# Loads from two queues, ternary weights ahead of the last head folds, and a fifth lane in the second layer of a post-norm decoder

## The reference

```python
x = _layernorm(x + _L0_attn_ref(x, weight, bias, decay_value))   # x @ (Wr + Wc) + bias; Wr, Wc upper triangular, made from powers of the decay
x = _layernorm(x + _L0_xattn_ref(x, ctx_512, Wq, Wkv_expand, Wout))  # 16 heads of 16 over 64 context rows, softmax
x = _layernorm(x + _L0_ffn_ref(x, router_w, gate_w, up_w, down_w, shared...))  # top 1 of 8 experts, and a shared expert
x = _layernorm(x + _L1_attn_ref(x, W_q, W_kv, W_o))     # FFT per head, L2 norm, cumulative sum over tokens, product, inverse FFT
x = _layernorm(x + _L1_xattn_ref(x, ctx_512, Wq, w_kc_q, w_kc_kv, W_qr, W_kr, Wo))  # 16 heads with rotary keys, softmax
x = _layernorm(x + _L1_ffn_ref(x, w_gate_up, w_proj))   # ternary weights, silu(gate) * up, rms norm
```

## Time and profile before

| | us |
|---|---|
| median of 3 runs (671.78 to 671.95) | 671.81 |
| the profiled execution, whole | 670.62 |
| its span, first to last instruction | 669.3 |
| PE busy, share of the span | 563.9, 84% |
| DVE busy | 477.3, 71% |
| ACT busy | 386.3, 58% |
| POOL busy | 378.5, 57% |

### The profile page before, as it was taken

One profiled execution on the slowest core, in us unless ns is written; L12 is line 12 of the kernel. 1 busy time (PEld: TensorE's weight loads), 2 busy tenths in 40 slices (PEclk: granted clock), 3 DMA queues, 4 the chain that ended last, 5 costly groups with the idle time before them and its releaser, 6 DMA issues. The chain is left out here.

```text
span 669.3 us, 14453 instructions
## 1 busy us (share of the span) xinstructions
PE 563.9 (84%) x5305; PEld 443.6 (66%) x5305; DVE 477.3 (71%) x1297; ACT 386.3 (58%) x826; POOL 378.5 (57%) x469
## 2 busy tenths in 40 slices
PE   3789998888798998906577999998999989999993
PEld 3566777777575655603345779786788777889982
DVE  3774757686578669549879665788688888777562
ACT  1767776766674554425544555682746747566552
POOL 3435374737751034259999896373654824444874
PEclk9999999999798999966769899999999999999997
DMA  7663222102553433261001010101000010000001
GB/s 231 191 213 88 76 71 74 49 2 84 164 168 116 137 103 116 72 181 40 28 26 35 1 32 3 32 1 33 1 7 27 2 32 1 1 1 3 1 17 47
DMA packets 50417, 41.96 MB, mean 63 GB/s; under 512 B 15514, under 2 KB 48796, under 8 KB 50332
## 3 DMA queue, kind: packets, MB, share of 16 engines
q1 hardware_dynamic: 48812, 36.85, 18.3%
q0 software_dynamic: 1536, 4.20, 1.9%
HBM read 31.72 MB, written 10.35 MB: 63 GB/s over the span
## 5 line engine op out<-in xcount | busy, mean ns | idle before, releaser
L1763 DVE TENSOR_TENSOR first<-bank,first 128x512 f16<-128x512 f32 (+3 forms) x141 | 75.5, 557 | 21.6 <-ACT first L1656 5.2
L2232 POOL TENSOR_TENSOR first<-first 128x512 f16<-128x512 f32 x44 | 51.8, 1180 | 33.9 <-ACT first L1650 27.1
L1039 PE MATMUL bank<-c_identity,first 128*128 128x128 f32 (+2 forms) x353 | 58.6, 281 | 14.4 <-ACT first L1589 3.2
L1039 PE MATMUL bank<-c_identity,wide 128*128 128x128 f32 (+3 forms) x203 | 35.8, 301 | 41.4 <-ACT wide L1589 20.7
L1032 PE MATMUL bank<-wide,first 128*128 128x256 f16 (+3 forms) x199 | 54.9, 286 | 4.7 <-DVE first L1763 2.4
L1039 PEld LDWEIGHTS bank<-c_identity,wide 128*128 128x128 f32 (+3 forms) x203 | 25.1, 151 | 48.3 <-ACT wide L1589 21.7
L1039 PEld LDWEIGHTS bank<-c_identity,first 128*128 128x128 f32 (+2 forms) x353 | 39.6, 139 | 23.8 <-ACT first L1589 4.2
L1033 PE MATMUL bank<-wide,first 128*128 128x256 f16 (+3 forms) x199 | 54.8, 285 | 0.0
L1034 PE MATMUL bank<-wide,first 128*128 128x256 f16 (+3 forms) x199 | 54.7, 285 | 0.0
L2210 POOL TENSOR_TENSOR first<-first,minus_half 128x2 f32<-128x2 f32 x30 | 22.0, 734 | 35.7 <-DVE first L1873 35.7
L1763 DVE TENSOR_TENSOR wide<-bank,wide 128x512 f16<-128x512 f32 (+3 forms) x57 | 35.1, 636 | 7.0 <-ACT wide L1629 2.2
(11 more groups left out here) (470 smaller groups left out, 2091.5 us busy)
## 6 DMA issues: line engine op xcount, KB each, us to landing
first<-sent_rows SPq DMA_DIRECT2D x20, 128.0 KB, 2.1
made_rows<-first SPq DMA_DIRECT2D x20, 128.0 KB, 1.7
wide<-in_L_xattn_Wq SPq DMA_DIRECT2D x9, 256.0 KB, 2.9
wide<-in_L_ffn_gate_w SPq DMA_DIRECT2D x8, 256.0 KB
wide<-in_L_ffn_up_w SPq DMA_DIRECT2D x8, 256.0 KB
wide<-in_L_ffn_down_w SPq DMA_DIRECT2D x8, 256.0 KB
wide<-in_L_xattn_Wo SPq DMA_DIRECT2D x16, 128.0 KB
wide<-in_L_ffn_w_gate_up SPq DMA_DIRECT2D x8, 256.0 KB
```

The source lines that it names most:

```text
L1039: last = nc.tensor.transpose(view[0:m, c0:c0 + n], src, kc["identity" if dt == F32 else "identity_bf"][0:n, 0:n])
L1763: return V.tensor_tensor(lo, whole, hi, ALU.subtract)
L2232: G.tensor_tensor(B.pl[r], B.pf, B.ph[r], ALU.subtract).then_inc(says("ex_l"), 1)
```

## The change

- **Loads.** A new part `ld_dv` loads the decay value and the steps on their own semaphore, first on SP; `pm_dv` and `pm_pow` wait for these two alone, `pm_diag` and `pm_b` for the seven transfers left in `ld_mix`. The copy of ones leaves `pm_pow` for a part `pm_one`. `ld_cross` and, for units 0 to 4, `ld` and `ld_ctx` are issued on ACT's queue; SP's remaining early loads are chained in a fixed order (constants, shared, spectrum, experts). The decay mask is bf16.
- **Turns.** The ternary weights come before the head folds 6 and 7.
- **Lane.** `LANES` is 5; the fifth lane lies over the stage buffers and the area `fifth`. The first unit in it, 12, waits in `gt`, `ld` and `ld_ctx` for `tb_tok`, all `fw_c` and all `ho_lo` (`staged`). Units take lane (u - 8) % 5.
- **Ternary scale.** Two DVE steps of `f_sc` become one.
- **Plan.** Several lengths are changed, and 60 passes are tried, not 30.

```diff
-LANES = 4
+LANES = 5
+STAGED = 4
-    c["decay_mask"] = (j >= i).astype(np.float32)
+    c["decay_mask"] = bf(j >= i)
-EARLY_FOLDS = 4
+EARLY_FOLDS, MIDDLE_FOLDS = 4, 6
-         + [("h", n) for n in range(EARLY_FOLDS, NPREP)] + [("f", n) for n in TERNARY])
+         + [("h", n) for n in range(EARLY_FOLDS, MIDDLE_FOLDS)] + [("f", n) for n in TERNARY] + [("h", n) for n in range(MIDDLE_FOLDS, NPREP)])
+def staged(u):
+    return NB <= u < NB + LANES and u - NB >= STAGED
-    p.add("ld_mix", 0, 0, "SP", 450, (), -10)
+    p.add("ld_dv", 0, 0, "SP", 90, (), -11)
+    p.add("ld_mix", 0, 0, "SP", 320, [("ld_dv", 0, 0)], -10)
-    p.add("ld_cross", 0, 0, "SP", 140, (), -8)
+    p.add("ld_cross", 0, 0, "ACT", 140, (), -8)
-    p.add("ld_const", 0, 0, "SP", 600, (), -7)
+    p.add("ld_const", 0, 0, "SP", 600, [("ld_mix", 0, 0)], -7)
-    p.add("pm_diag", 0, 0, "DVE", 87, [("pm_pow", 0, 0)], -10)
+    p.add("pm_diag", 0, 0, "DVE", 102, [("pm_pow", 0, 0), ("in_mix", 0, 0)], -10)
-            p.add("ld_e", 0, i, "SP", 140, freed, rank)
+            p.add("ld_e", 0, i, "SP", 140 if i > 1 else 230, freed if i > 1 else [("ld_spec", 0, 0)], rank)
-            p.add("f_sc", 0, i, "DVE", 160, [("f_16", 0, i)], rank)
+            p.add("f_sc", 0, i, "DVE", 170, [("f_16", 0, i)], rank)
-        p.add("ld", u, 0, "SP", 45, [old("res", 2), old("rt_xs")], -9.5 + 0.01 * u if u < FIRST else k)
+        p.add("ld", u, 0, "ACT" if u < FIRST else "SP", 45, [old("res", 2), old("rt_xs")], -9.5 + 0.01 * u if u < FIRST else k)
+        if staged(u):
+            gate += [("tb_tok", 0, 0)] + [(name, 0, n) for name in ("fw_c", "ho_lo") for n in range(NPREP)]
-    p.settle(8, 30)
+    p.settle(8, 60)
-            pool_ = [couples[n - 2].back()]
+            pool_ = [couples[n - 2].back()]
+        else:
+            pool_ = [wide.back(STAGES), fifth.back()]
-        return k.B[u % FIRST if u < NB else FIRST + u % LANES]
+        return k.B[u % FIRST if u < NB else FIRST + (u - NB) % LANES]
+        if staged(u):
+            sp.wait_ge(*done("tb_tok", 0))
+            for i in range(NPREP):
+                sp.wait_ge(*done("fw_c", 0, i))
+                sp.wait_ge(*done("ho_lo", 0, i))
+    def load(out, in_, s):
+        nc.scalar.dma_start(out, in_).then_inc(s, 16)
-        dve.step(V.tensor_scalar(W.sc16, W.sc32, 1.0 / GRP, None, ALU.mult))
-        dve.step(V.tensor_scalar(W.sc16, W.sc16, 1e-8, None, ALU.max))
+        dve.step(V.tensor_scalar(W.sc16, W.sc32, 1.0 / GRP, 1e-8, ALU.mult, ALU.max))
+        pool.wait_ge(*done("tb_tok", 0))
+        if staged(u):
+            for n in range(NPREP):
+                pool.wait_ge(*done("fw_c", 0, n))
+                pool.wait_ge(*done("ho_lo", 0, n))
```

More of the change, by code:

```diff
@@ L847, in turns_of, with later_turns @@
     return len(range(n, NB, FIRST))
+def later_turns(n):
+    return sum((u - NB) % LANES == n for u in range(NB, 2 * NB))
 def sync_program(k, sp):
@@ L955, in ld @@
                 sp.wait_ge(*done("ln_x", u - LANES, 3))
-            load(B.y, unit_rows(k.x_mid, u - NB), dma["x"][u % LANES])
+            load(B.y, unit_rows(k.x_mid, u - NB), dma["x"][(u - NB) % LANES])
     def ld_ctx(u, g):
-        B, s = k.lane(u), dma["ctx"][u % FIRST if u < NB else u % LANES]
+        B, s = k.lane(u), dma["ctx"][u % FIRST if u < NB else (u - NB) % LANES]
         if u >= NB:
@@ L992, in st @@
         sp.wait_ge(*done("ln_x", u, 3))
[L993 to L995 removed]
+        load(unit_rows(k.out, u - NB), k.lane(u).x, dma["lane_out"][(u - NB) % LANES])
+    parts = {f.__name__: f for f in (ld_dv, ld_mix, ld_const, ld_shared, ld_spec, ld_zero, ld_tab, ld_e, ld_h, ld_f, ld, ld_ctx, st_mid, x_ld,
                                      x_st, st)}
@@ L1482, in summed, with ld_cross, ld, ld_ctx @@
         return summed_rows(k, u, n)
+    def load(out, in_, s):
+        nc.scalar.dma_start(out, in_).then_inc(s, 16)
+    def ld_cross(u, g):
+        for out, name in ((pre.raw_t[0], "L0_xattn_Wq"), (pre.raw_t[1], "L0_xattn_Wout"), (pre.raw_kv, "L0_xattn_Wkv_expand")):
+            load(out, k.A[name].rearrange("(c p) n -> p c n", p=P), dma["cross"])
+    def ld(u, g):
+        load(lane(u).x, k.A["x"][u:u + 1, :, :].rearrange("a (t p) n -> p (a t) n", p=P), dma["x"][u])
+    def ld_ctx(u, g):
+        for half in range(2):
+            load(lane(u).ctx[half * L:(half + 1) * L, :], k.A["ctx_512"][u, :, :], dma["ctx"][u])
     def pm_hi(u, g):
```

110 lines of the change are left out of this document (56 added, 54 removed).

## The result

| | before | changed |
|---|---|---|
| median, 6 runs each, us | 671.79 (666.96 to 672.66) | 662.63 (661.06 to 664.98) |
| the profiled execution's span, us | 669.3 | 662.0 |

The ratio of changed to before is 0.988 (95% interval 0.985 to 0.992). The forecast was 647 with a range of 632 to 664: the sign is right, the time is in the range, and the size is off by a factor of 2.7.

What follows compares the result with a forecast made beforehand. The span was taken as PE's busy time plus its 105.4 us idle; -3.9 - 2 - 13.6 - 5 = -24.5 on 669.3 gave 644.8. With the median 2.5 above the span, the forecast was 647, range 632 to 664.

Steps and rivals of the forecast that it cites:

- start: Before the first mixing product: x issued first on ACT's queue brings that product near 19.8 us, 3.9 us earlier.
- rest of the first layer: First layer after the first mixing product: reordered, taken at 0 (-4 to +4).
- experts: Experts' stage: two folds leave, four ternary units come, the bound goes from PE to DVE: -2 us (-9 to +6).
- rival D: Experts' stage: DVE becomes the bound, units' waits and SP's queue add 8 to 12 us; 658 total, chance 0.11.
- rival F: Experts' stage: each ternary unit's DVE steps wait out whole POOL steps, 46 us in seven units; 687 total, chance 0.06.
- Hand-over: Between layers: norm's power 1.8 us earlier, fold 6 fills 3.9; PE idle until the first turn 19.0 to 13.3.
- Filling: Second layer's first units, 304.2 to 400: 16 POOL steps leave, PE idle 22.9 to 10 (5 to 18).
- rival C: Second layer's filling: fold 7 late, PE and POOL stand before unit 8's q; 660 total, chance 0.08.
- parts 2 and 3: Experts' stage -2 us, and hand-over with filling of the second layer -13.6 us.
- Lane: Second layer, 400 to 580: unit 12 loads some 60 to 90 us earlier, halving PE's 10.6 idle: -5 (0 to -9).
- rival G: Whole kernel: the new order uses none of the freed time, or several rivals meet; 672 total, chance 0.03.
- E: Start: yields nothing, since the same bytes share the same engines or ACT's issues are slow; 651 total, chance 0.07.

Runs made afterwards that it cites:

- before_first_of_after: Kernel before with only the changed kernel's first-layer order on the four computing engines (very first parts, folds 6 and 7 free): 674.9 us, ratio 1.008.
- after_first_of_before: Changed kernel with the parts ahead of the experts' first tile kept in the kernel before's order on the four computing engines: 656.3 us.
- only_loads: Kernel before with the load edits alone, including the bf16 mask and merged scale step; four lanes, old turns and lengths: 675.4 us, ratio 1.008.
- old_loads_150: Whole change but the loads (all on SP as before), with 150 planner passes: 644.2 us, ratio 0.961 to the kernel before.
- fixed_old_loads: old_loads_150 with the whole order of its four computing engines written out and 4 planner passes: 643.4 us.
- fixed_new_loads_free_start: fixed_old_loads with the new loads instead, and the first parts placed by the planner for them: 644.1 us.

## Why the prediction was wrong, point by point

| term | forecast | in the two profiles |
|---|---|---|
| start | -3.9 | -3.0 |
| rest of the first layer | 0 (-4 to +4) | +18.2 |
| experts | -2 (-9 to +6) | +7.0 |
| hand-over, filling, lane | -18.6 | -29.5 |
| sum | -24.5 | -7.3 |

**The step that failed** is the sentence "The rest of the first layer, reordered, I take at 0 (-4 to +4)". It had no row behind it. Behind the start the diff changes no instruction of that stretch, only lengths and passes by which the planner orders it, and I took the reordering for noise around zero; but PE's order there differs in nearly every unit, and a stretch of 184 us in which three engines are two thirds busy or more has room for much more than 4 us. What stood in its place is +18.2 us, of which some 16 are the order alone (before_first_of_after, after_first_of_before). What in the change made the planner choose that order stays open: only_loads, with the old lengths and 30 passes, has a first layer of 203.6 us already, and no run changed the lengths alone.

**The start.** Right in its dates, only partly in its cause. ACT's table load comes after its 18 transfers, its first activation stands where the forecast wanted it (12.3):

```profile
11.32 1.28 ACT L1632 ACT_TABLE_LOAD   x1 [11.32 <-issue]
12.61 0.60 ACT L1632 ACTIVATE first<-bank 128x512 f16<-128x512 f32 x1
```

The first product is at 20.69 (forecast 19.8, has 23.69). But most of the gain is not the loads': old_loads_150 starts at 21.0 without them, by standing the first turn ahead of the spectrum, and between fixed_old_loads and fixed_new_loads_free_start they give 1.1 us (20.4, 19.3). And in no run did it reach the total, since the earlier start is eaten behind it. The sentence on the Trainium skill (DMA: Bandwidth & Descriptors, Rules for kernel authors) gave 0 for the same term; the fixed versions, with 643.4 and 644.1, side with it in the total.

**The experts.** The forecast had PE freed of 9 us in this stage. It was not: 70.75 us busy against 70.50. Cut at the first rows, the stage before held only one and a half folds (the first products of fold 6, at 205.29, stand ahead of it), 6.7 us of fold products; the changed one has the end of fold 5, 3.8 us. The ternary transposes rose from 1.3 us (18 of them) to 3.8 (42). DVE got 12.7 us more (67.45 against 54.71), where 15.4 were forecast, and at 76% it was no full engine; it cost time all the same, by standing ahead of tiles' steps in its own order. A share of busy time doesn't tell that. The experts' last product is at 306 us, where 279 was forecast. That is rival D in place and nearly in size (its +8 to +12; +7.0 came), at a chance of 0.11. What D named as the mechanism, waits beside POOL's steps, was there but small, in the groups by line of the two small steps:

```profile
L1885 DVE TENSOR_SCALAR wide<-wide 128x12 bf16<-128x12 f32 x7 | 3.9, 555 | 0.2
L1886 DVE TENSOR_SCALAR wide<-wide 128x12 f32<-128x12 bf16 x7 | 2.6, 370 | 0.2
```

The means hide that nearly all of these 14 steps took 0.17 us; three, in three units, took 1.27, 1.55 and 1.59, each until a POOL step beside it ended. One of them:

```profile
297.24 1.59 DVE L1885 TENSOR_SCALAR wide<-wide 128x12 bf16<-128x12 f32 x1
...
297.17 1.64 POOL L2316 TENSOR_TENSOR wide<-wide 128x768 bf16<-128x768 bf16 x1
```

That is 4 us in seven units. Before, it was 2.4 in three, all in one unit (steps of 1.28 and 1.49 us). The rule of the Trainium skill (Advanced Engine Details and Errata, VectorE Performance Modes) agrees with these rows in kind; rival F's 46 us did not come, since most steps fell into POOL's pauses.

**Hand-over.** As forecast, counted from the first gather: eight gathers, then the power 10.3 us after the first (forecast 10.1), and fold 6 in the hole, whose load ends PE's idle time:

```profile
322.19 3.73 PE L1126 MATMUL bank<-wide 128*96 128x256 f32 x8 [11.93 <-DMA wide<-in_L_xattn_W_qr]
```

From the first gather to the first spectral product PE is idle for 10.2 us, 15.9 before: the 5.7 that were forecast.

**Filling.** From 326 to 400 POOL is busy for 60.5 of 74.0 us, 82% where under 75 was forecast (93% in the earlier trace rows); PE is idle for 13.5 where 10 was put, 7.4 of it in one piece:

```profile
365.75 0.47 PE L1058 MATMUL bank<-c_identity,wide 128*128 128x128 f32 x1 [7.38 <-ACT wide L1623]
```

That is turn 8.1, which waits for unit 8's second norm. Fold 7's products end at 355 (forecast 330), ahead of it, and so held up nothing but themselves: of rival C only the date was right. The turns as a whole, in the fixed order, gave 9.5 us where parts 2 and 3 had 15.6: they took 6.3 among the experts, where the forecast had -2. The size that was too small is the one behind: with the clock at 0.98 instead of 0.94, PE's work behind the spectral product fell by 11.9 us although fold 7 had moved in. The forecast had 4.

**Lane.** Forecast -5, measured -7.0 with the order held fixed. Unit 12 loads where it should:

```profile
360.34 0.40 SPq L875 DMA_DIRECT2D wide<-x_mid  x1
```

48 us behind the first gather, not 139. In the 180 us from 400 PE is idle for 5.0 us (forecast under 6), and the tail fell too, from 11.9 to 6.8 idle, which was taken at 0. In the changed kernel itself the lane does not show: its version with four lanes is 5.2 faster, with another order of the first layer.

**The chances.** The forecast's cases held several of the mechanisms, but none of them had the planner make a worse order where the diff changes no instruction; rival G touched on it ("the new order uses none of the freed time") at 0.03. That the time lies in the range is luck: the range's upper half was there for other mishaps (C, D, E), and the errors of 18 us in the first layer and 9 among the experts were partly cancelled by 11 us more gain behind them than forecast.

## What to carry to other kernels

Where a planner orders the whole program, an edit has two effects, its own and that of another order everywhere else, and here the second was the larger (17 to 18 us against 7 to 10 for each part). Cut both orders at the same events before forecasting, and price every stretch whose order changed, also where the diff is silent. To measure a part, hold the order fixed: with the whole order kept, the second layer came out within 0.4 us in four versions; with the first layer's alone kept, that layer came within 2 to 5 us; without it, removing the lane or keeping only the loads moved it by 9 and 19. And let the planner search longer before a change is judged: 150 passes instead of 60 gave 8 us here.

## What the runs showed of the hardware

Filling PE's waits raised the granted clock from 0.91 to 0.97 over 200 us and made PE's own work 12.5 us cheaper, and the layer took 202.7 us instead of 202.6. I had counted PE's busy time as a part of the path, since the span is its busy plus its idle time; in the 75 us behind unit 7's load the two traded one for one (5.1 us less work of its own, 8.1 of fillers, the same length), because another engine set the pace. In such a stretch work on PE that fits into its waits cost nothing, and making PE's work cheaper won nothing. Where the fillers stood behind a wait, ahead of 109 us, they did cost 1.4 us.

A step of VectorE on 12 numbers per partition, 0.17 us by itself, took up to 1.62 us when it met a step of GpSimd, and then ended with it. The experts' steps that read a PSUM bank took 0.42 us in both kernels.
